# Layer 2's score matmuls rotate through two PSUM banks in place of three

## The reference

```python
scores = jnp.einsum('bhqd,bhkd->bhqk', q, k) * scale
attn = jax.nn.softmax(scores, axis=-1)
ctx = jnp.einsum('bhqk,bhkd->bhqd', attn, v)
...
out = jnp.einsum('bhwc,dc->bhwd', ctx, Wo) + bo
```

## Time and profile before

| | |
|---|---|
| time, median of 3 runs | 526.73 us (526.36 to 528.58) |
| span of the profiled execution | 528.0 us |
| PE busy, share of the span | 439.1 us, 83% |
| DVE busy | 342.4 us, 65% |
| ACT busy | 288.9 us, 55% |
| POOL busy | 132.8 us, 25% |
| layer 2's loop, first score to last exponential | about 233 to 341 us |

### The profile page before, as it was taken

The page is one execution under the profiler, slowest core; times in us unless marked ns, Lnnn a source line. Parts: engine busy times, 40 slices in busy tenths (PEclk is TensorE's granted clock), DMA queues, the critical chain, the costliest instruction groups (busy, mean ns, idle before and its releaser), DMA issues. The chain is left out here.

```text
span 528.0 us, 9368 instructions
## 1 busy us (share of the span) xinstructions
PE 439.1 (83%) x3406; PEld 231.3 (44%) x3406; DVE 342.4 (65%) x668; ACT 288.9 (55%) x511; POOL 132.8 (25%) x162
## 2 busy tenths in 40 slices
PE   0527768899999887679999999939898999999995
PEld 0216648555455664223333333324443454454442
DVE  4549876233344568978999996251654778777784
ACT  1279955131532437047878778722865578486441
POOL 4420004000000005744422212031364428065000
PEclk9956997999999988559999999957977999999999
DMA  5500000900000004952200000016390480933302
GB/s 142 164 0 1 0 0 1 197 1 1 0 1 0 1 0 107 279 175 67 73 27 3 3 2 4 0 47 160 100 226 15 89 181 2 217 55 68 67 2 79
DMA packets 20767, 33.79 MB, mean 64 GB/s; under 512 B 5657, under 2 KB 15497, under 8 KB 19957
## 3 DMA queue, kind: packets, MB, share of 16 engines
q1 hardware_dynamic: 16724, 23.70, 18.9%
q0 software_dynamic: 2176, 6.35, 4.3%
q10 hardware_dynamic: 1824, 3.19, 2.3%
HBM read 16.21 MB, written 4.64 MB: 39 GB/s over the span
## 5 line engine op out<-in xcount | busy, mean ns | idle before, releaser
L1335 DVE TENSOR_TENSOR L_s<-L_row_ps,L_cols 128x1024 f32<-128x1024 f32 x72 | 87.6, 1218 | 9.3 <-PE L_row_ps L1500 7.5
L910 DVE TENSOR_REDUCE L_mx<-L_ring 128x2 f32<-128x512 f32 x128 | 83.3, 686 | 12.4 <-PE L_ring L1034 11.8
L965 ACT ACTIVATE L_e<-L_ring 128x512 f32<-128x512 f32 x128 | 73.7, 597 | 21.4 <-PE L_ring L1047 19.3
L1523 PE MATMUL L_acc<-L_s,L_t_sb 128*64 128x256 f32 x576 | 81.6, 406 | 1.1 <-DVE L_s L1335 1.0
L1404 ACT ACTIVATE L_cols<-L_col_ps 128x512 f32<-128x512 f32 x72 | 42.8, 596 | 48.9 <-PE L_col_ps L1510 48.5
L1034 PE MATMUL L_ring<-stacks_k_st,stacks_q_st 64*128 64x256 bf16 x256 | 51.0, 301 | 7.0 <-DMA stacks_k_st<-L_k_parts 4.7
L1523 PEld LDWEIGHTS L_acc<-L_s,L_t_sb 128*64 128x64 f32 x576 | 36.0, 140 | 35.9 <-DVE L_s L1335 19.8
L1047 PE MATMUL L_ring<-stacks_q_st,stacks_k_st 64*128 64x256 bf16 x256 | 47.2, 282 | 1.2 <-DMA stacks_q_st<-L_m_parts 1.2
L1500 PE MATMUL L_row_ps<-L_hats,L_sel 48*128 48x512 bf16 x144 | 44.6, 392 | 0.0
L1067 PE MATMUL L_ctx_ps<-L_e,L_v_x 128*32 128x256 f32 x512 | 41.5, 398 | 0.0
L1311 DVE COPY L_t_sb<-L_acc 128x192 f32<-128x192 f32 x48 | 17.1, 357 | 31.4 <-PE L_acc L1491 31.4
(11 more groups left out here) (270 smaller groups left out, 814.2 us busy)
## 6 DMA issues: line engine op xcount, KB each, us to landing
L_hats<-L_parts SPq DMA_DIRECT2D x28, 216.0 KB, 5.0
L_hat<-L_offsets SPq DMA_DIRECT2D x20, 192.0 KB, 4.7
L_mask<-L_offsets SPq DMA_DIRECT2D x10, 192.0 KB, 4.9
stacks_q_st<-L_q_parts SPq DMA_DIRECT2D x12, 128.0 KB, 3.9
stacks_k_st<-L_k_parts ACTq DMA_DIRECT2D x12, 128.0 KB, 4.8
stacks_q_st<-L_q_parts POOLq DMA_DIRECT2D x12, 128.0 KB, 2.7
stacks_k_st<-L_k_parts POOLq DMA_DIRECT2D x12, 128.0 KB, 2.9
L_stack<-L_xpad SPq DMA_DIRECT2D x7, 162.0 KB, 5.8
```

Source lines behind the costliest of these rows:

```text
L910: dve.tensor_reduce(mx[:, n % 2, :, head], ring[:, place(step) % 3].rearrange("p (q s) -> p q s", q=2), AX.X, ALU.max).then_inc(max_read, 1)
L965: act.activation(e[:, k], ring[:, 3 + v % 3], ACT.Exp, scale=HD2 ** -0.5).then_inc(e_ready, 1)
L1335: dve.tensor_tensor(s[:, q], row_ps[:, q], cols[:, t % 3:t % 3 + 1].broadcast_to([P, 2, 2 * N]), ALU.mult).then_inc(s_ready, 1)
L1523: mm = pe.matmul(acc[C * e:C * e + C, b, 0:N], t_sb[:, b, h, (KK * e + t) * C:(KK * e + t + 1) * C], s[:, q, h, e * N:(e + 1) * N], start= ...
```

## The change

The second pass uses banks 3 and 4 of `ring` in turn. Bank 5 is then used only ahead of the loop. The wait of the score matmuls goes with it: score step v waits for the exponential of step v - 2, where it waited for that of step v - 3. Nothing else is changed; the instructions are the same in kind and number.

```diff
@@ layer2, scalar: exponents(v)
-                    act.activation(e[:, k], ring[:, 3 + v % 3], ACT.Exp, scale=HD2 ** -0.5).then_inc(e_ready, 1)
+                    act.activation(e[:, k], ring[:, 3 + v % 2], ACT.Exp, scale=HD2 ** -0.5).then_inc(e_ready, 1)
@@ layer2, tensor: scores(v)
-                    if v > 2:
-                        pe.wait_ge(e_ready, v - 2)
+                    if v > 1:
+                        pe.wait_ge(e_ready, v - 1)
                     for t in range(2):
-                        mm = pe.matmul(ring[:, 3 + v % 3, t * N:(t + 1) * N], rows_of(k_st, c, h, p)[:, t * P:(t + 1) * P], rows_of(q_st, c, h, p),
+                        mm = pe.matmul(ring[:, 3 + v % 2, t * N:(t + 1) * N], rows_of(k_st, c, h, p)[:, t * P:(t + 1) * P], rows_of(q_st, c, h, p),
                                        start=True, stop=True)
```

## The result

The changed kernel takes 528.95 us (median of 15 runs, 527.62 to 531.67), the kernel before 526.68 us (15 runs, 525.44 to 528.87). The ratio is 1.0042 with a 95% interval from 1.0024 to 1.0060: between 1.3 and 3.2 us slower. The forecast was 527.9 us with a range from 526.5 to 530.3.

The account below looks back on a forecast made before the run. PE's written order with short waits was taken to bound layer 2's loop. Image 0's 0.49, image 1's 0.68 and 0 for the rest made 1.17 us, so 526.73 became 527.9 us, range 526.5 to 530.3.

Parts of the forecast that it names:

- score(0,6) late: Image 0 at half the clock: two banks limit the scores, so this one starts at 236.94, not 236.03, 0.91 us late.
- `turn_maxima` of image 0 late: Image 0: it follows the held score(0,6) at 237.48 instead of waiting for DVE till 236.67, 0.81 us late.
- image 0 longer, clock rise unmoved: Image 0: its last context step falls behind the unmoved clock rise, so image 1 starts 0.49 us late.
- image 0 longer, its last context step at half the clock: Image 0, upper bound: the clock rise moves along with the delay, so the loss is 0.81 us.
- image 1 longer: Image 1, full clock: score(1,5) waits for exp(1,3) with no addition covering it; 0.68 us lost, bounds 0.3 and 0.81.
- images 2 to 15: Full clock: only score(c,5) is held, hidden behind `turn_context`'s wait; nothing booked, upper bound 1.8 us.
- round of a bank: Image 0 at half the clock: exponential 0.60, release 0.05, score to exponential 0.67, together 1.32 us for two steps.
- the cover: Images 2 to 15: `turn_context`'s wait for DVE's addition hides score(c,5)'s 0.13 us hold, with 0.03 us to spare.
- The rule of the skill: Using all eight PSUM banks speaks against the change; read as a price in every image, the sum is 3.0 us.
- The clock as a rival: Loop start: PE stands still more, so the clock may rise an image later; 2.8 us, up to 4; chance 10%.
- The prediction's own signs: Loop: 8 to 25 score waits, at most 6 us; score(0,6) 0.9 late; score(1,5) 0.05 behind exp(1,3); images 2-15 within 0.5.
- signs of being wrong: Images 2 to 15 growing 0.1 us each, clock at 0.50 beyond image 0, or later layers changing over a microsecond.

Follow-up runs that it names:

- without the cover: Kernel before and changed kernel, each with DVE's addition reading x, not the projected context, and `turn_context` not waiting for it; 521.28 and 525.79 us, one run each.
- changed, again: The changed kernel unaltered, measured once more beside the kernel before; 528.81 us (12 runs), ratio 1.0029 (1.0008 to 1.0050).

## Why the prediction was right

Side by side, in us. The pair of full kernels had the clock rise 6.5 and 6.4 us after score(0,0), as the prediction assumed. That it did is luck: the rise moves from one execution to the next (see the clock below).

| step of the prediction | forecast | measured |
|---|---|---|
| score(0,6) late | 0.91 | 3.88 - 3.02 = 0.86 |
| `turn_maxima` of image 0 late | 0.81 | (236.84 - 232.43) - (236.67 - 233.01) = 0.75 |
| image 0 longer, clock rise unmoved | 0.49 | 7.06 - 6.68 = 0.38 |
| image 0 longer, its last context step at half the clock | 0.81 | 0.71 (7.50 against 6.79, without layer 3) |
| image 1 longer | 0.68 | 6.30 - 5.65 = 0.65 |
| images 2 to 15 | 0 | -0.02 |
| wait of score(c,5) hidden by the addition | 0.13 | 0.14, hidden |
| loop | 1.17 | 1.0 |
| time | 1.17 | 2.3 (1.3 to 3.2), then 1.6, without layer 3 1.1 |

**Image 0.** The round of a bank was right: 1.32 us forecast, 1.29 measured. The release took 0.06 us, and from a held score's start to its exponential's it took 0.64 to 0.65 us in place of 0.67. `turn_maxima` followed score(0,6) by 0.53 us (forecast 0.54), and score(0,7) came 2.07 us after score(0,6) in place of 2.22, as DVE no longer held PE up there.

**Image 1.** Right in mechanism and size. With image 1 alone on two banks it was 0.66 us again up to score(1,7). Where the half clock lasts into image 1 the term is smaller: without layer 3 image 1 took 6.30 us against 5.84, 0.46 more, and image 0 0.71 more. The two together lose about the same.

**Images 2 to 15.** The riskiest step, since the cover was computed at 0.03 us. It held in all profiles with two banks and the first pass unchanged (95.74 to 95.77 us). The removal of the addition shows that it hides the wait in every second image and in the last two; in the others the wait of `turn_maxima` for DVE would hide it too, which the prediction didn't see. The single bank shows the bank's round as the governing quantity.

**The rule of the skill.** Trainium skill, Perfetto Trace Analysis, section Matmul Optimizations, asks for all eight banks in use. Here the trace agrees in direction only. The third bank is worth 1.0 to 1.1 us in 108, all of it at the loop's start; the second is worth 32 us in images 2 to 15 (127.85 against 95.74).

**The clock as a rival.** It is partly right. Nine profiles, in order of the clock's rise, with three banks in images 0 and 1 and then with two (the addition that two of them leave out doesn't fall into these images):

| banks in images 0 and 1 | clock rise after score(0,0) | images 0 and 1 together |
|---|---|---|
| 3 (before, without the cover) | 5.0 | 11.72 |
| 3 (before) | 6.5 | 12.33 |
| 3 (before, no layer 3) | 7.2 | 12.63 |
| 3 (two banks from image 2 on) | 8.0 | 13.27, of it 0.30 at the seam |
| 2 (changed) | 6.4 | 13.37 |
| 2 (changed, no layer 3) | 7.4 | 13.81 |
| 2 (changed, without the cover) | 7.6 | 13.84 |
| 2 (changed, again) | 7.7 | 13.89 |
| 2 (first pass with four banks) | 10.0 | 14.89 |

With the seam taken off (12.97), the rows of three banks lie on a line of 0.42 us for each us of a later rise: 11.72 + 0.42 x 3.0 = 12.98. Against this line the four changed kernels with rises from 6.4 to 7.7 lose 1.0 to 1.1 us each. So the loss by the banks is the same at each of these rises, and a rise 2.5 us later costs as much again.

Whether two banks also make the rise later is open. In the eleven profiles without extra matmuls and with at least two banks, it came after 3.4, 5.0, 6.5, 7.2 and 8.0 us with three banks in image 0, and after 6.4, 7.1, 7.4, 7.6, 7.7 and 10.0 with two (the last with another first pass). The means are 6.0 and 7.7 us. Of all ways to split these eleven numbers, 6 in 100 give as large a lead, so it may be chance. If it is real, it is worth 1.7 x 0.42 = 0.7 us on top of the 1.0. The mean granted clock of the whole runs doesn't show it: beside each other it was 0.913 in the 12 runs of the changed kernel and 0.911 in the 30 of the kernel before, where 1.7 us more at half the clock would lower it by 0.002.

**The time.** The forecast of 1.17 us lies just below the first interval (1.3 to 3.2) and inside that of the second comparison (0.4 to 2.6). Behind the loop the full kernels with two or three banks took between 183.5 and 187.5 us for the same program, so more than three times the effect lies in noise there. In the profiled pair that noise even turned the sign of the span. What of the first comparison's 2.3 us is more than the loop's 1.0 stays open, between chance, a later rise and the layer behind: image 0 alone on two banks measured 2.2 us with an interval from 0.6 to 3.8, which can't tell it either. The pair without layer 3 gives 1.1 us, with ranges of 2.2 us each, and speaks weakly against a larger effect inside the first three layers.

**The prediction's own signs.** Of what it said would show it, all came: 10 waits and 4.0 us, score(0,6) 0.86 us late, score(1,5) 0.06 us behind exp(1,3), images 2 to 15 unchanged. But two of its signs of being wrong came as well. The layers behind the loop changed by 1.1 us in the profiled pair, more than the microsecond that it allowed, and in the second profile of the changed kernel the clock stayed at 0.50 beyond the first image (7.7 us against 7.51). Both also happen between profiles of three banks (behind the loop 186.9 and 183.6 us with the extra matmuls; a rise at 7.2 us in an image 0 of 6.79), so they were drawn too narrowly to tell anything about the change.

One number of the prediction was set wrongly: it put the profiled span of 528.0 beside the median of 526.73, as if 1.3 us lay between. A run of the changed kernel that spans 527.4 us takes 529.15, so 1.75 us lie around the span. The profiled execution of before, had it the same around it, would take some 529.8, longer than any of the 15 runs. The sum, a difference, doesn't depend on it.

No version here beats the kernel before.

## What to carry to other kernels

Work out a bank's round (consumer's duration, release, producer's start to the consumer's start) and divide it by the number of banks: where that is below the step of whatever paces the loop, one bank fewer costs nothing on average. Then look for places where the loop issues two steps in one go, and ask what PE waits for next: a held score of 0.14 us was free here in image after image, because the very next instruction had to wait for something else until 0.03 us later. The start of a loop, where the usual filling work is missing, is where the spare buffer earned its place; without the addition the end was another. And when an experiment mixes two rotations, look at the seam between them: here it added a wait of 0.3 us that belonged to neither.

## What the runs showed of the hardware

- The granted clock (0.50, the 1.2 GHz level, to 1.00, the 2.4 GHz level) rose at another moment in each profile: 3.4 to 8.0 us after score(0,0) with three banks in image 0, for the same PE program up to there. Image 0 took 5.49 us with the rise at 3.4 us, 6.68 with 6.5 and 6.79 with 7.2 and 8.0.
- The mean granted clock alone doesn't tell a stretch's time: behind the loop, the same program took 183.5 and 186.5 us in two executions with the same mean clock of 0.92 there (image 1 alone on two banks; the changed kernel once more). What makes up the 3 us was not looked for.
- More matmuls ahead of the loop brought the full clock earlier, and it was lost again 0.5 to 1.7 us after the first score. In the 3.2 us up to the fall PE was busy 2.00 us, with a standstill for the DMA of the maxima in it:

```profile
229.50:232.70 3.20, 2.00 (x22) 1.31 (x23) 2.34 (x4) 1.66 (x2) 2.47 (x7) 1.00 0.47 128
```

- In the same loop, images 2 to 13 repeated in two lengths, 6.69 and 7.13 us, equal to 0.01 us through the whole loop and in both kernels, and the stretch from score(2,0) on came out between 95.74 and 95.77 us in ten profiles. So a difference of 0.05 us can be read there from a single profile, where the interval from 15 runs of the whole program is 1.9 us wide.
